# Last layer of a four-layer transformer: tokens of three batches grouped by their chosen experts, the last batch computed by all experts

## What is computed

```
gate_logits = xf @ w_gate
topk_logits, topk_idx = jax.lax.top_k(gate_logits, TOP_K)
gates = jax.nn.softmax(topk_logits, axis=-1)
cw = jnp.sum(jax.nn.one_hot(topk_idx, NUM_EXPERTS, dtype=xf.dtype) * gates[..., None], axis=1)
hmid = jax.nn.gelu(jnp.einsum('tc,ech->eth', xf, w1) + b1[:, None, :], approximate=True)
eo = jnp.einsum('eth,ehc->etc', hmid, w2) + b2[:, None, :]
moe = jnp.einsum('te,etc->tc', cw, eo).reshape(B, N, C)
return x + g_mlp[:, None, :] * moe
```

## Time and profile before

| | us |
|---|---|
| median of 3 runs (lowest, highest) | 1894.54 (1894.29, 1901.86) |
| the profiled execution | 1896.54 |
| its span | 1894.1 |
| PE busy | 1738.4 (92%) |
| DVE busy | 1159.2 (61%) |
| ACT busy | 914.4 (48%) |
| POOL busy | 577.1 (30%) |

### The profile page before, as it was taken

How to read it: one execution, slowest core, us unless ns; L and a number is a source line. 1 busy time by engine, 2 the same in 40 slices (tenths; PEclk the granted TensorE clock), 3 DMA queues, 4 the chain that set the end, 5 groups by cost and what they waited for, 6 DMA issues and landing times.

```text
span 1894.1 us, 27931 instructions
## 1 busy us (share of the span) xinstructions
PE 1738.4 (92%) x9838; PEld 1141.3 (60%) x9838; DVE 1159.2 (61%) x2573; ACT 914.4 (48%) x1635; POOL 577.1 (30%) x567
## 2 busy tenths in 40 slices
PE   6775899998998889998899999999999999999998
PEld 2443444433796634443378764444388899999997
DVE  7863677773555667677436567777445645455454
ACT  2323476667354468675745247676733322222221
POOL 4432122214555323332435232222523301101000
PEclk9997699999999889899899999998999899999999
DMA  7202333331001222323100223333110000100000
GB/s 245 79 2 71 95 105 91 91 112 48 11 1 51 91 82 72 90 70 114 57 11 1 88 67 109 92 100 114 39 38 19 20 25 20 44 10 29 1 26 25
DMA packets 65866, 116.49 MB, mean 61 GB/s; under 512 B 9443, under 2 KB 25235, under 8 KB 65439
## 3 DMA queue, kind: packets, MB, share of 16 engines
q1 hardware_dynamic: 65728, 114.71, 19.6%
HBM read 83.46 MB, written 30.73 MB: 60 GB/s over the span
## 4 chain that ended last, share of the span: by engine, by line
PE 70%; DVE 10%; ACT 7%; issue 4%; DMA 4%; POOL 4%; SPq 2%; DVEq 0%; ACTq 0%; POOLq 0%
PE ps L1696 25%; PE ps L1780 15%; PE ps L1749 8%; PE ps L1735 7%; PE ps L1844 6%; PE ps L1717 5%; ACT Pr L1545 2%; DMA heads_t<-stage 2%; PE ps L1820 1%; DVE negmax L1133 1%; ACT HQ L1520 1%; DVE GT L1059 1%; ACT act L1519 1%; ACT xn L1441 1%; PE ps L1586 1%
## 5 line engine op out<-in xcount | busy, mean ns | idle before, releaser
L1133 DVE TENSOR_REDUCE negmax<-ps 128x1 f32<-128x512 f32 x768 | 488.3, 681 | 221.3 <-PE ps L1717 218.0
L1545 ACT ACTIVATE Pr<-ps 128x512 f32<-128x512 f32 x768 | 410.6, 602 | 208.3 <-PE ps L1735 208.0
L1556 ACT ACTIVATE g<-ps,b1col 128x512 f32<-128x512 f32 x216 | 148.2, 688 | 449.1 <-PE ps L1696 445.0
L1322 DVE CAST G<-g 128x512 fp32r<-128x512 f32 x216 | 122.8, 568 | 280.7 <-ACT g L1556 280.2
L1735 PE MATMUL ps<-QK 55*128 55x512 f32 x768 | 239.5, 515 | 33.4 <-ACT Pr L1545 25.2
L1780 PE MATMUL ps<-W2a,G 128*128 128x288 f32 x1728 | 263.4, 302 | 4.8 <-DVE rowt L1143 4.8
L1780 PEld LDWEIGHTS ps<-W2a,G 128*128 128x128 f32 x1728 | 247.9, 192 | 19.1 <-DVE G L1324 7.3
L1749 PE MATMUL ps<-Pr,V 128*32 128x512 f32 x1536 | 220.0, 646 | 0.0
L1717 PE MATMUL ps<-QK 54*128 54x512 f32 x768 | 196.6, 444 | 18.7 <-DVE negmax L1133 7.0
L1735 PEld LDWEIGHTS ps<-QK 55*128 55x128 f32 x768 | 92.2, 192 | 198.7 <-ACT Pr L1545 103.5
L1324 DVE TENSOR_TENSOR G<-g,G 128x512 fp32r<-128x512 f32 x216 | 170.4, 789 | 7.4
(11 more groups left out here) (221 smaller groups left out, 2241.1 us busy)
## 6 DMA issues: line engine op xcount, KB each, us to landing
QK<-heads_t SPq DMA_DIRECT2D x192, 144.0 KB
heads_t<-stage SPq DMA_DIRECT2D x96, 252.0 KB
QK<-heads_t SPq DMA_DIRECT2D x192, 72.0 KB
raw<-in_w SPq DMA_DIRECT2D x18, 432.0 KB
raw<-in_w SPq DMA_DIRECT2D x12, 576.0 KB
WA<-in_ada_w SPq DMA_DIRECT2D x3, 1728.0 KB
heads_t<-stage SPq DMA_DIRECT2D x24, 144.0 KB
QK<-W1a SPq DMA_DIRECT2D x192, 2.0 KB
```

The lines of the kernel that those rows point to most:

```text
L1133: dve.tensor_reduce(negmax[:, m % 2, h, t:t + 1], ps[:, row_bank(l, s, i), :], AX, ALU.max, negate=True).then_inc(a_free, 1)
L1322: dve.tensor_copy(G[:, n % 3, 0, :], g32[:, n % 2, :]).then_inc(g_hi, 1)
L1545: act.activation(Pr[:, t % 2, 2 * half + pair, :], ps[:, (16 * s + u) % 3, :], ACT.Exp, scale=SCALE).then_inc(b_free, 1)
L1556: act.activation(g32[:, n % 2, :], ps[:, hidden_bank(s), :], ACT.Gelu if l == 1 else ACT.Gelu_apprx_tanh, bias=b1col[:, e, s % FT:s % FT + ...
```

## The change

The 1536 tokens of batches 0 to 2 are no longer computed by every expert. Their normalisation, gate and choice (`choices`) move into the attention on batches 2 and 3. DVE ranks each token among those with the same expert (a matmul with a triangular matrix), POOL writes each modulated token as a row of 352 floats into a DRAM tensor once for each of its two experts by indirect DMAs (`scatter`), into regions of 1536 rows an expert. The 3072 rows fill at most nine tiles of 512 rows, however they fall on the experts; a table of the expert and first row of each tile is made on DVE and read by SP into registers. Each of the nine grouped windows loads its tile (`xg`), transposes it (`lng`, no shift and scale) and stores its result in DRAM (`store`). The four windows after that compute batch 3 by all experts as before, and in windows 9, 10 and 11 POOL gathers two result rows for each token of one batch (`gather`), DVE weighs and adds them (`merge`). So there are 13 windows in place of 16. Every window has its own weights, in the two buffers in turn, so all six pieces are loaded and split in each window but the last. The DRAM tensor of rows (7680 x 352) is filled with zeros in the prologue by one DMA, on which SP waits at the prologue's end. The last layer's first two `hidden` no longer run inside the attention.

The core of the diff (left out: semaphores, buffers, DVE's `rank`, `table`, `slots` and `merge`, which are chains of small operations):

```diff
 EARLY = 2
-EBASE = [sum(EXPERTS[:l]) for l in range(LAYERS + 1)]
+LAST, SEL = LAYERS - 1, B - 1
+GROUPED = 2 * SEL + EXPERTS[-1] - 1
...
-for _e in range(1, EXPERTS[-1]):
-    PIECES += [("w1", LAYERS - 1, _e, c) for c in range(3)] + [("w2", LAYERS - 1, _e, c) for c in range(3)]
+for _v in range(1, WINDOWS[-1]):
+    PIECES += [("w1", LAST, _v, c) for c in range(3)] + [("w2", LAST, _v, c) for c in range(3)]
...
+    out = []
+    if b == 1:
+        out += [(6, "setup", l, 0, 0), (12, "wg", l, 0, 0)]
+    if b == 2:
+        out += [(12 + t, "stats2", l, 0, t) for t in range(TT)] + [(17, "mean2", l, 0, 0)]
+        out += [(10, "modrow", l, 0, 0), (24, "mod", l, 0, 0)] + [(26 + c, "ln2", l, 0, c) for c in range(3)]
+        out += [(30, "gate", l, 0, 0), (32, "gexp", l, 0, 0), (33, "weigh", l, 0, 0), (33, "rank", l, 0, 0), (34, "scatter", l, 0, 0)]
+        out += [(22 + t, "stats2", l, 1, t) for t in range(TT)] + [(26, "mean2", l, 1, 0), (26, "modrow", l, 1, 0)]
+    if b == 3:
+        out += [(2 + c, "ln2", l, 1, c) for c in range(3)] + [(9, "mod", l, 1, 0)]
+        out += [(13, "gate", l, 1, 0), (14, "gexp", l, 1, 0), (15, "weigh", l, 1, 0), (15, "rank", l, 1, 0), (17, "scatter", l, 1, 0)]
+        out += [(t, "stats2", l, 2, k) for k, t in enumerate((8, 10, 12, 13))] + [(14, "mean2", l, 2, 0), (14, "modrow", l, 2, 0)]
+        out += [(19 + c, "ln2", l, 2, c) for c in range(3)] + [(19, "mod", l, 2, 0)]
+        out += [(22, "gate", l, 2, 0), (23, "gexp", l, 2, 0), (24, "weigh", l, 2, 0), (24, "rank", l, 2, 0), (25, "scatter", l, 2, 0)]
+        out += [(25, "table", l, 0, 0), (28, "xg", l, 0, 0)]
+        first = PIECE["w1", l, 0, 0]
+        out += [(t, "load", l, first + q, 0) for q, t in enumerate((0, 0, 5, 9, 13, 23))]
+        out += [(t, "split", l, first + q, 0) for q, t in enumerate((4, 8, 12, 21, 23, 27))]
     return out
...
-def expert_window(l, v):
-    e, b = divmod(v, B)
+def grouped_window(l, v):
     out = [(4, "fin", l, v - 1, 0)] if v > 0 else []
+    if 0 < v <= GROUPED:
+        out += [(5, "store", l, v - 1, 0)]
     if v == 0:
-        out += leaving(l)
-    if e == 0:
...
-                n = first + 2 * (b - 1) + q
-                out += [(t - 6, "load", l, n, 0), (t, "split", l, n, 0)]
-    if v == EXPERTS[l] * B - 1:
+        out += [(0, "out", l, STEPS - 1, 0), (0, "turn", l, STEPS - 1, 0)]
+        out += [(0, "proj", l, B - 1, t) for t in range(TT)]
+        out += [(0, "lng", l, 0, c) for c in range(3)] + [(6, "slots", l, 0, 0), (8, "b2", l, 0, 0)]
+    if v == 1:
+        out += [(t // 2, "stats2", l, B - 1, t) for t in range(TT)] + [(2, "mean2", l, B - 1, 0)]
+        out += [(8 + c, "ln2", l, B - 1, c) for c in range(3)]
+    if v == 2:
+        out += [(3, "gate", l, B - 1, 0), (5, "gexp", l, B - 1, 0), (7, "weigh", l, B - 1, 0)]
+    if v + 1 < WINDOWS[l]:
+        first = PIECE["w1", l, v + 1, 0]
+        out += [(t, "load", l, first + q, 0) for q, t in enumerate((0, 0, 7, 8, 11, 12))]
+        out += [(t, "split", l, first + q, 0) for q, t in enumerate((5, 6, 9, 10, 13, 14))]
+        out += [(9, "side", l, v + 1, 0)]
+    if v + 1 < GROUPED:
+        out += [(1, "xg", l, v + 1, 0)] + [(11 + 2 * c, "lng", l, v + 1, c) for c in range(3)]
+    for b in range(SEL):
+        if v == GROUPED + b:
+            out += [(8, "gather", l, b, 0), (14, "merge", l, b, 0), (16, "merge", l, b, 1)]
+    if v == WINDOWS[l] - 1:
         out += [(21, "fin", l, v, 0)]
     return out
...
+            def tile_load(l, v):
+                sp.wait_ge(xs_out, ALL_XS)
+                if v >= 2:
+                    sp.wait_ge(misc_full, MISC["lng", l, v - 2, 2] + 1)
+                row = 0
+                if v > 0:
+                    sp.wait_ge(table_ready, 1)
+                    row = sp.value_load(tab[0:1, 1, v - 1:v], min_val=0, max_val=XROWS - N)
+                sp.dma_start(XG[v % 2][:, :, :], tok_rows[bass.ds(row, N), :].rearrange("(t p) c -> p t c", p=128)).then_inc(xg_in[v % 2], 16)
+            def tile_store(l, v):
+                sp.wait_ge(acc_free, TT * (WBASE[l] + v + 1))
+                sp.dma_start(exp_rows[N * v:N * v + N, :].rearrange("(t p) c -> p t c", p=128), rowt[:, :, :]).then_inc(ys_out, 16)
...
+                if PIECES[n][:3] == ("w2", LAST, 0):
+                    pool.wait_ge(xs_out, 16 * 2 * TT * 2)
+                    pool.wait_ge(mod_done, SEL)
                 high = hi if low.start == 0 else hi[64:low.stop]
...
+                elif kind == "mod":
+                    mb = MB[i // 2]
+                    pool.wait_ge(xn_ready, NORM["mean2", l, i, 0] + 1)
+                    pool.wait_ge(modr_in, 32 * (i + 1))
+                    if i == 1:
+                        pool.wait_ge(xs_out, 16 * 2 * TT)
+                    if i == 2:
+                        pool.wait_ge(misc_full, hq_over(l, B - 1))
+                    pool.tensor_tensor(mb[:, :, :], xn[:, :, :], bc3(modr[:, 1, :], TT), ALU.mult).then_inc(pool_done, 1)
+                    pool.wait_ge(pool_done, pool_step())
+                    pool.tensor_tensor(mb[:, :, :], mb[:, :, :], bc3(modr[:, 0, :], TT), ALU.add).then_inc(mod_done, 1)
+                    pool.wait_ge(mod_done, i + 1)
+                elif kind == "scatter":
+                    pool.wait_ge(zero_out, 16)
+                    pool.wait_ge(idx_ready, i + 1)
+                    for t in range(TT):
+                        for r in range(2):
+                            pool.indirect_dma_start(tok_rows, bass.IndirectOffsetOnAxis(idx[:, i, t, r:r + 1], 0),
+                                                    MB[i // 2][:, t, :], None).then_inc(xs_out, 16)
+                    pool.wait_ge(xs_out, 16 * 2 * TT * (i + 1))
+                elif kind == "gather":
+                    pool.wait_ge(ys_out, 16 * GROUPED)
+                    pool.wait_ge(slots_ready, 1)
+                    pool.wait_ge(misc_full, MISC["lng", l, GROUPED - 1, 2] + 1)
+                    if i > 0:
+                        pool.wait_ge(merged, i)
+                    for t in range(TT):
+                        for r in range(2):
+                            pool.indirect_dma_start(XG[r][:, t, 0:C], None, exp_rows,
+                                                    bass.IndirectOffsetOnAxis(yidx[:, i, t, r:r + 1], 0)).then_inc(yg_in, 16)
+                    pool.wait_ge(yg_in, 16 * 2 * TT * (i + 1))
                 elif kind == "gexp":
...
+                        if what == "mean2" and pl == LAST and pb < SEL:
+                            act.wait_ge(mod_done, pb + 1)
                 act.activation(xn[:, t, 0:C], X[:, TT * b + t, :], ACT.Identity, bias=shift[:, t:t + 1],
                                scale=rstd[:, t:t + 1]).then_inc(xn_part, 1)
```

479 lines of the change are left out of this document (385 added, 94 removed).

## The result

| | before | changed |
|---|---|---|
| median (lowest, highest), 4 runs each on one chip, us | 1898.2 (1894.3, 1904.8) | 1947.8 (1943.8, 1956.4) |
| span of the profiled execution | 1894.1 | 1948.3 |
| PE, DVE, ACT, POOL busy | 1738, 1159, 914, 577 | 1708, 1228, 975, 815 |

The changed kernel is slower: ratio 1.0264, 95% interval 1.0213 to 1.0314. The forecast was 1875, its range ended at 1928. The rows that answer to the earlier trace rows are these windows of the changed kernel: the attention on batches 2 and 3, from the last exponential to the first gelu, then the expert windows 0, 1, 2, 3 to 7, 8, 9 to 11 and the last (columns as there).

The account below looks back on a forecast made before the run. Expert windows were taken as PE-bound, three fewer worth 87 us; attention, gathers, transposes and lows took most back. The stretch summed to 519.5 against 538.7 us, 19.2 less, giving 1875 us, range 1843 to 1928.

Parts of the forecast that it names:

- group of eight DMAs, G: POOL's time to issue eight indirect DMAs and wait for their landing: 7.0 + 3.0 = 10.0 us, six groups in all.
- batch 2's window, more: Attention on batch 2 gets batch 0's choice; with DVE loaded, it was to grow by 3 us.
- batch 3's start to the first expert tile: Attention on batch 3: POOL's 81.6 us list sets the length, first expert tile 95 us after the start, before 63.
- window 0, 1, 2: First expert windows, with PE's clock after its wait, batch 3's normalisation and its gate: 36.4, 35.6 and 41 us.
- windows 3 to 7, each: Grouped expert windows: three transposes and a 1.2 us wait of PE for the last low, 31.4 us each.
- window 8: Expert window without a gather: 29.1 us, as the windows before the change.
- windows 9 to 11, each: Expert windows with a gather that delays low, load, split and gelu: PE waits 7.7 us, loses 4 to clock, 40.8 each.
- The price of an issue: POOL's time to issue one indirect DMA: taken as 0.88 us, forecast case 0.6 to 1.15, nothing gained from 1.28.
- The landing: Wait at the end of a group of POOL's indirect DMAs: 3.0 us, taken from SP's output write.
- The rival that DVE blocks POOL's issues: Expert windows: DVE's subtractions and casts make POOL's issues wait, a third more on G, 1895 us; chance 0.10.
- the rival of the late weight chain: Weight pieces land 1 us later, making a grouped window 3 us longer, eight times: 1899 us; chance 0.10.
- the fill in the prologue: Zero fill of the DRAM rows, 32 us from 70 us on, done at 102: costed at nothing.

Follow-up runs that it names:

- e4: The changed kernel with seven of the eight DMAs of each scatter left out, most expert-tile rows staying zero: 1930.1 us, ratio 1.017.
- e11: e10, with DVE taking POOL's token lows, additions to X and some products in the last attention window: 1871.2 us, ratio 0.986.
- e5: The changed kernel with batch 3's four projections at ticks 6 to 12 of the first expert window, behind the first tile's transposes: 1936.11 us, ratio 1.020.
- e7: The changed kernel with the choices of batches 0 and 1 some 22 and 13 ticks earlier in the last attention: 1951.7 us, ratio 1.031.
- e1: The changed kernel with weight pieces split and loaded, and the next tile transposed, at earlier ticks in each expert window: 1937.35 us, ratio 1.018.
- e2: The changed kernel with each gather behind its window's last weight low and the merges in the next window: 1928.06 us, ratio 1.015.
- e6: The changed kernel with the expert windows' low parts on DVE instead of POOL, and merges in the window behind the gather: 1887.97 us, ratio 0.9963.
- e8: The changed kernel with each expert window's weight splits in three spaced pairs, loads and transposes moved, POOL's work the same: 1916.2 us, ratio 1.008.
- e10: The changed kernel with the moves of e6 and e5 together and the merges at ticks 12 and 16: 1875.83 us, ratio 0.988.
- e14: e12 with 30 more PE matmuls, whose result nothing reads, late in the last attention: 1868.2 us, ratio 0.984.
- e16: The changed kernel with the 30 idle matmuls of e14 and nothing else: 1950.83 us, ratio 1.029.
- e13: The changed kernel with gates of batches 0 to 2 by 7 matmuls of 16 columns, not 28 of 4, on 128 tokens alone: 1938.2 us, ratio 1.021.
- e17: e12 with 12 wide matmuls, whose result nothing reads, among the 28 of every gate in the last layer: 1875.89 us, ratio 0.989.
- e12: e11 with batch 2's two passes for the modulated tokens on DVE instead of POOL: 1865.43 us, ratio 0.983.

## Why the prediction was wrong

By its own steps, forecast and measured, in us:

| step | forecast | measured |
|---|---|---|
| group of eight DMAs, G | 10.0 | 11.6 to 12.3 |
| batch 2's window, more | 3 | 10.6 |
| batch 3's start to the first expert tile | 95 | 137.6 to its first matmul, 142.4 to its gelu |
| window 0, 1, 2 | 36.4, 35.6, 41 | 33.2, 38.2, 40.6 |
| windows 3 to 7, each | 31.4 | 34.0 |
| window 8 | 29.1 | 29.4 |
| windows 9 to 11, each | 40.8 | 41.3 |

**The step that failed is the one on the attention on batch 3.** It took POOL's list of 81.6 us, with some 3.6 us of waits, as the thing that sets the length, let ACT be "pulled along", and priced PE's clock there at nothing. The list itself was right: POOL was busy 71.4 us, and its scatters held it for another 11 between their issues and for their landings, so some 82. But the window was 111.3, and POOL waited in the other 29: 8.2 us for DVE's `idx`, 6.6 for `ptmp`, 5.1 for `tmp`, 4.1 for `rsum`, steps that waited for PE in their turn. So the last scatter had landed 112 us after the window's start and not 85, and the first tile's first matmul came 25.4 us behind it and not 10.

What the runs show of the length: the prediction's DMAs (e4, 21 us for seven eighths of them), PE's two waits of 8 us behind scatters and passes, worth 12 (e11), which is part of the same; the projections in front of the first tile, 12.5 (e5), which the prediction did not count; and the cost goes with each choice, wherever it stands (e7). PE was also busy 27 us longer, mostly at half clock, 72 us of it in one piece in the profiled execution. I had the 8 us of half clock of the earlier trace rows before me and used them for windows and not here. That the clock made the window longer by as much is not shown: seven kernels have the same code there (changed, e1, e2, e5, e6, e8, e10), and their window took 111.0 to 111.9 us, whether the mean clock was 0.62 and PE busy 84.9 or 0.68 and PE busy 80.8. Where the clock was higher, PE waited more.

**Batch 2's window** was to be 3 us longer and was 10.6. PE was busy 9.4 us longer in it, for the transposes and the gate of batch 0 and for 8.8 us of half clock from 1323.9 on. The forecast had looked at DVE alone.

**The price of an issue** was 0.96 in the rows, inside 0.6 to 1.15, but the step from one to the next is 1.27, just at the 1.28 from which I had said that nothing is gained. The landing, 1.6 to 2.3, was shorter than the 3.0 forecast. By the 6 us per us of G, the whole is 10 us or a little more. The rival that DVE blocks POOL's issues had a mechanism that exists (see the last section) but hardly a price in the changed kernel, where DVE has no long subtractions beside them: the 24 of the scatters took 0.958 to 1.226 us, median 0.960, those of the gathers 0.942 to 1.123.

**Windows 3 to 7** are the rival of the late weight chain, at 2.6 us each where it had 3. Pieces landed 3.1 to 4 us after their load, POOL's lows of w2 took 2.05 to 2.5 us (median 2.3) where the forecast had 2.12, and the last low came 1.5 us later than forecast (32.8 us after the window's first matmul against 31.3). So PE waited 2.15 to 2.73 us, with 3.4 us of half clock behind three of the five waits. The forecast had taken 1.2 us and no clock. e8 and e6 show the cause.

**Right** were window 8, the fill in the prologue, and in window 9 the gather's mechanism link by link. The closeness of 41.3 to 40.8 is in part luck: PE waited 9.3 to 10.0 us where 7.7 were forecast, half clock cost some 2.4 where 4 were, and in windows 10 and 11 3.0 us of the wait are for DVE beside POOL's lows, which no term had. The first windows agree as a sum (112.0 against 113.0) and not one by one. The merges were costed at nothing; e2 shows that they are not, once they run beside POOL's lows.

**Open** is why PE's clock stays at the lower level in this stretch, when before it stood at 1.00 from 1338.8 to the stretch's end. It is neither that PE has too little to do late in it (e14, e16), nor the gates' narrow matmuls (e13, e17), nor the waits behind POOL alone (e11). Nothing else was tried. By busy time and mean clock it is most of the 27 us that PE was busy longer; what the window would take at full clock is open too.

## What to carry over

Moving small steps into a stage where four engines already wait for one another costs more than the sum on the busiest of them: price each place where an engine in order stands behind a long one, and put what blocks for long (here eight indirect DMAs, 12 us) on an engine for whose list nobody waits. In a chain through two buffers, space the pieces by a low part plus a landing, rather than start the chain earlier: the same work in three pairs took a window from 34.0 to 30.6 us. The grouping pays once such things are mended: e12, with POOL's lows on DVE and the first tile ahead of the projections, is 1.7% faster than the kernel before (ratio 0.977 to 0.988). e8's spacing was not combined with it.

## Unexpected of the hardware

- POOL's running subtraction held DVE's casts, multiplications and additions until it ended: four multiplications 6.05 us in place of 1.20, four additions into X 6.62 in place of 1.80, casts 1.15 in place of 0.42 on average. POOL's own subtraction over 128x1152 took 2.67 to 3.00 us there, against 2.64 in the attention. The Trainium skill (SBUF — State Buffer, Who interferes with whom) says that casts and tensor-scalar forms can take a port pair shared with POOL and that the one that issues first fully blocks the other. These rows agree. The prediction had cited it for the other direction.
- That other direction shows too, one DMA at a time. In e6 the gathers' DMAs ran beside DVE's low parts and took 0.94 to 1.84 us each, median 1.08, against a median of 0.946 in the changed kernel. Each of e6's eight that took over 1.2 us began while DVE worked on operands in SBUF, and ended 0.82 us (once 0.98) after DVE's operation. A group of eight grew by 0.7 to 2.4 us by it. Timeline of DVE and POOL in e6, one such pair, and then the line of the gathers' DMAs (ns, minimum, median, maximum):

```profile
1767.99 1.35 DVE L1598 TENSOR_TENSOR W1a<-raw,W1a 32x1152 fp32r<-32x1152 f32 x1
1768.36 1.80 POOL L1202 DMA_INDIRECT XG<-exp_rows,yidx  x1 [0.30 <-issue]
...
L1202 POOL DMA_INDIRECT XG<-exp_rows,yidx x24: 942/1080/1842, 1765.0 to 1846.4; - x24
```

- PE busy 95% of 100 us and still a granted clock of 0.64 (e14).
